# Rows of y in groups of four steps, and transposes with TensorE's transpose flag, in a state-space layer with a gated feed-forward

## The chip, the cores and the metric

The kernel runs on one core of a Trainium2 chip. The metric is the device time of one execution in microseconds (us). TensorE, VectorE, ScalarE and GpSimd each have their own instruction stream and meet by semaphores; in the profile they are PE (its weight loads PEld), DVE, ACT and POOL, and SP only issues transfers.

## The reference, cut to what matters

Two sequences of 1024 steps, width D = 512, state N = 128 per channel; the feed-forward has 2048 hidden units.

```
xn = rmsnorm(x) * norm_w;  xn = xn * sigmoid((xn @ select_w.T + b) * gate)
delta, B, C = split(xn @ x_proj_w.T);  delta = softplus(delta @ dt_w.T + dt_b)
for each step:  h = exp(delta * A) * h + (delta * xn) outer B;  y = h . C
x = layernorm(x + (y + x * D_param) @ out_w.T)
x = layernorm(x + (silu(x @ w_gate.T) * (x @ w_up.T)) @ w_down.T)
```

The scan over steps is the only sequential part: h of one step needs h of the step before.

## The kernel before, in words

All data are float32. The 128 partitions hold the state index N; the free axis holds the two sequences times 512 channels, so h of one step is 128 x 1024 in a ring of seven slots (`H_RING = 7`). The 1024 steps are cut into 8 chunks of 128 (`TB`), and into blocks of four steps (`BS = 4`).

- VectorE (line 693 on) runs the recurrence. Per step and sequence it multiplies `a` (the decay) by the h before into PSUM (`m_ps`, L708), and adds the input term into the next slot of h (L728 where the input term was scaled beforehand, L731 where this is part of the same instruction). Before it writes h of step t it waits at L713 for `s_y >= t - H_RING + 1`, that is for the row of y of step t-7, because that row reads the slot to be overwritten.
- TensorE gives the exponents: `exponents(q)` (L1214, matmuls at L1223) spreads delta times A for half a block into four PSUM banks, and ScalarE takes the exponential from there into `a` (L1004). Its places are in the table `P_AT`, one at every odd step. It needs ScalarE to have read the one before.
- TensorE gives the rows of y: `y_row(t)` (L1287) multiplies h of step t by a column of C placed so that the result falls into one row of `y_ps`; four column groups of the array are used, two by even and two by odd steps. It waits for h of its own step and adds one to `s_y`. A float32 matmul leaves two records, so two steps have eight records of L1299.
- Everything else is hung on the steps by `timetable`: for each half step a list of pieces of the chunk before (output projection, layer norm, gate and up products, down product) and of the chunk after (the projections that give delta, B, C). TensorE issues the pieces of a half step behind the exponents and the rows of y placed there, strictly in that order, so a wait in one holds up all that follows. Sixteen windows of 64 steps are projected and normalised; ScalarE copies `y_ps` at the second step behind each window, and the first row of the next window waits for that; windows of y (`yt`) and of the first norm's output (`vt`) are transposed by four matmuls against the identity (L1123 and L1163).
- Weights stream from HBM through `w_ring`, each load issued by ScalarE when TensorE has used up the slot; SP issues the broadcast of the input term of each step (`u_bc`).
- After the last step the second half of the last chunk is finished alone (the tail), in which VectorE does the norms and copies.

Of the kernel before, what the change touches and what calls it, by code (L numbers as in the profile page):

```python
# [5 lines left out]
BATCH, SEQ, D, N, R, HID = 2, 1024, 512, 128, 128, 2048  # L6
# [11 lines left out]
BS = 4  # L18
# [175 lines left out]
def build(nc, xT, x_rows, vecs, d_row, sel_wT, xproj_wT, dt_wT, out_wT, A_log, gu_w, down_w, out_rows):  # L194
# [5 lines left out]
    with ctx:  # L200
# [855 lines left out]
        def tensor(e):  # L1056
# [52 lines left out]
            def behind(x, stage, j):  # L1109
                cols = columns_of(x)  # L1110
                if stage == "yt":
# [6 lines left out]
                    for k in range(KB):  # L1118
                        if x > LAST and k % PAIR == 0:
                            e.wait_ge(s_y2, k // PAIR + 1)  # L1120
                        part = dst if x <= LAST else final_half(stage, x, j, k // PAIR)
                        at = k if x <= LAST else k % PAIR
                        last = e.matmul(part[:, at * P:(at + 1) * P], v(x, j)[:, k * P:(k + 1) * P], ident[:, :], start=True,  # L1123
                                        stop=True)
                        if x > LAST and k % PAIR:
                            last.then_inc(s_yt2, 1)
                    if x <= LAST:
# [24 lines left out]
                elif stage == "vt":  # L1152
# [3 lines left out]
                    for k in range(KB):  # L1156
                        if x > LAST and k == 0:
                            e.wait_ge(s_nm, 1)
                        elif x > LAST and k == PAIR:
                            e.wait_ge(s_work, emptied("outp", x, j))  # L1160
                        part = dst if x <= LAST else final_half(stage, x, j, k // PAIR)
                        at = k if x <= LAST else k % PAIR
                        last = e.matmul(part[:, at * P:(at + 1) * P], v(x, j)[:, k * P:(k + 1) * P], ident[:, :], start=True,  # L1163
                                        stop=True)
                        if x > LAST and k % PAIR:
                            last.then_inc(s_vt2, 1)
                    if x <= LAST:
# [13 lines left out]
                elif stage == "down":  # L1181
# [13 lines left out]
                    for i in range(HB // 4):  # L1195
                        hb = part * (HB // 2) + sub * (HB // 4) + i
                        if m == 0:
                            e.wait_ge(s_gated, HB // 2 * x + hb // 2 + 1)
                        last = e.matmul(dst, tile[:, sub * (HB // 4) + i, :], hidden(x, hb), start=hb == 0,  # L1199
                                        stop=hb == HB - 1)  # L1200
# [86 lines left out]
            def y_row(t):  # L1287
                blk, i = t // CS, t % WIN // 2
                if t == 0:
                    e.wait_ge(s_ucp, BATCH * FIRST_U)  # L1290
                elif t % WIN == 0:
                    e.wait_ge(s_ycp, t // WIN)
                e.wait_ge(s_cz, blk + 1)
                e.wait_ge(s_h, BATCH * (t + 1))
                for b in range(BATCH):
                    entry = (blk % CZ_RING * BATCH + b) * CS + t % CS
                    first = GP * entry + GP - 1 - i
                    group = 2 * (t % 2) + b
                    last = e.matmul(y_ps[group * GP:(group + 1) * GP, :], cz[:, first:first + GP],  # L1299
                                    h[:, t % H_RING, b * D:(b + 1) * D], start=i == 0, stop=i == GP - 1)  # L1300
                last.then_inc(s_y, 1)

            first_chunk()
            for t in range(SEQ):
                c = t // TB
                for i in range(SLOTS):
                    if SLOTS * t + i in P_AT:
                        exponents(P_AT[SLOTS * t + i], p_ps)
                    if i == 0 and t % 2 == 0 and t:
                        y_row(t - 2)  # L1310
                        y_row(t - 1)
                    for stage, x, j in plans[c].get(SLOTS * (t % TB) + i, ()):
                        behind(x, stage, j)
                        before(x, stage, j)
            y_row(SEQ - 2)
            y_row(SEQ - 1)
            e.wait_ge(s_exp, TILES_P)
            for slot in sorted(plans[CHUNKS]):
                for stage, x, j in plans[CHUNKS][slot]:
# [50 lines left out]
```

## Time and profile before

| | us |
|---|---|
| three timed runs | 2670.43, 2664.76, 2670.15 (median 2670.15) |
| span of the profiled execution, first to last instruction | 2662.4 |
| the profiled execution's time around its span | not given by the page; the runs lie 2.4 to 8.0 above the span |
| VectorE busy / TensorE busy / ScalarE busy / GpSimd busy | 2577.2 / 2323.3 / 1836.4 / 1030.8 |
| scan, first step to last step | 37.4 to 2599.4 |
| tail behind it | 63 |

Times are from the start of the span. Busy shares are averages over stages with different limits; a row of the timeline has its start, its duration, the engine, the line, what is written and read, the count of merged records, and in brackets the idle time of the engine before it with what ended it. The granted clock of TensorE has two levels, full (2.4 GHz) and half (1.2 GHz).

### The profile page before, as it was taken

To read this page: it belongs to the slowest core of one execution; us is meant where nothing else is said; L and a number is where in the kernel's file an instruction comes from. 1 tells how busy PE (TensorE), PEld (TensorE's weight loads), DVE (VectorE), ACT (ScalarE), POOL (GpSimd) and SP (SyncE) were. 2 spreads that over 40 slices of the span, in tenths; PEclk is the share of its full clock that TensorE was granted. 3 is DMA by queue.
4 is the path that set the end of the run, shared out by engine and by line. 5 is a ranking of instruction groups with operands and counts; after the bars stand their busy time and mean duration, and the time that the engine had idled before them with its cause. 6 is when DMAs were issued, how large, how long until landed. Compare 5 with 4: busy or idle time off the path is not lost.

```text
span 2662.4 us, 48762 instructions
## 1 busy us (share of the span) xinstructions
PE 2323.3 (87%) x17036; PEld 1281.6 (48%) x17036; DVE 2577.2 (97%) x4160; ACT 1836.4 (69%) x2432; POOL 1030.8 (39%) x1031
## 2 busy tenths in 40 slices
PE   7867678999789987899889998899978998998898
PEld 4322234545345544555445553454534554465557
DVE  6999999999999999999999999999999999999892
ACT  5778767678676776667766777767867678653743
POOL 2343333443344433444334433344334443343320
PEclk8999999999899998999999999999989999999999
DMA  5666666777667776777767787677766777787784
GB/s 189 216 215 223 225 237 238 276 257 275 239 243 272 269 270 228 252 268 276 264 231 264 258 287 246 233 278 257 271 245 231 272 265 268 264 289 281 246 323 156
DMA packets 192064, 672.20 MB, mean 252 GB/s; under 512 B 20944, under 2 KB 26064, under 8 KB 191824
## 3 DMA queue, kind: packets, MB, share of 16 engines
q1 hardware_dynamic: 152432, 544.02, 57.8%
q10 hardware_dynamic: 39392, 125.06, 13.8%
q8 instruction: 140, 2.29, 0.3%
q14 instruction: 100, 0.82, 0.1%
HBM read 660.61 MB, written 8.39 MB: 251 GB/s over the span
## 4 chain that ended last, share of the span: by engine, by line
PE 45%; DVE 25%; ACT 14%; issue 11%; DMA 4%; DVEq 0%; ACTq 0%; POOL 0%; POOLq 0%
PE banks L1059 14%; PE banks L1223 11%; DVE h L731 11%; PE banks L1299 9%; DVE banks L708 9%; PE banks L1199 8%; ACT a L1004 6%; DVE h L728 5%; DMA U<-in_xT 2%; ACT L742 1%; ACT u_bc L1023 1%; DMA u_bc<-u_scratch 1%; PE banks L1151 1%; PE banks L1147 1%; DMA w_ring<-in_down_w 1%
## 5 line engine op out<-in xcount | busy, mean ns | idle before, releaser
L708 DVE TENSOR_TENSOR banks<-a,h 128x512 f32<-128x512 f32 x2048 | 1331.5, 692 | 6.9 <-ACT a L1004 6.9
L1004 ACT ACTIVATE a<-banks 128x2048 f32<-128x2048 f32 x512 | 960.3, 1876 | 510.1 <-PE banks L1223 464.8
L731 DVE SCALAR_TENSOR_TENSOR h<-u_bc,BCt,banks 128x512 f32<-128x512 f32 x1285 | 899.0, 734 | 5.9 <-PE banks L1299 5.8
L603 POOL TENSOR_TENSOR dexp<-spread,dt 128x512 f32<-128x512 f32 x512 | 538.5, 1052 | 815.2 <-DVE banks L708 765.7
L1299 PE MATMUL banks<-h,cz 128*32 128x512 f32 x4096 | 696.7, 618 | 97.6 <-DVE h L728 50.0
L1223 PE MATMUL banks<-dexp,A 32*128 32x256 f32 x8192 | 612.1, 414 | 149.6 <-ACT a L1004 147.8
L1223 PEld LDWEIGHTS banks<-dexp,A 32*128 32x128 f32 x8192 | 383.9, 191 | 474.7 <-ACT a L1004 354.5
L728 DVE TENSOR_TENSOR h<-u_bc,banks 128x512 f32<-128x512 f32 x763 | 489.8, 674 | 3.3 <-POOL u_bc L615 3.3
L1059 PE MATMUL banks<-vT,w_ring 128*128 128x256 f32 x1792 | 453.2, 396 | 18.7 <-ACT up L971 17.6
L1059 PEld LDWEIGHTS banks<-vT,w_ring 128*128 128x128 f32 x1792 | 326.0, 192 | 187.7 <-issue 108.8
L1023 ACT ACTIVATE u_bc<-u_bc,BCt 128x512 f32<-128x512 f32 x497 | 333.2, 713 | 61.7 <-DMA u_bc<-u_scratch 60.9
L615 POOL TENSOR_SCALAR u_bc<-u_bc,BCt 128x512 f32<-128x512 f32 x266 | 184.0, 692 | 379.7 <-DVE banks L708 379.7
L1299 PEld LDWEIGHTS banks<-h,cz 128*32 128x32 f32 x4096 | 109.0, 109 | 382.5 <-issue 370.0
L1199 PE MATMUL banks<-gated,w_ring 128*128 128x256 f32 x896 | 225.1, 394 | 16.0 <-ACT vT L976 8.9
L1199 PEld LDWEIGHTS banks<-gated,w_ring 128*128 128x128 f32 x896 | 162.1, 191 | 100.1 <-issue 65.4
L969 ACT ACTIVATE sg<-banks 128x256 f32<-128x256 f32 (+1 forms) x144 | 51.8, 360 | 143.4 <-PE banks L1059 141.9
L543 POOL TENSOR_TENSOR gated<-gated,sg 128x512 f32<-128x512 f32 x56 | 75.0, 1340 | 96.1 <-DVE banks L708 75.5
L546 POOL TENSOR_TENSOR gated<-gated,up 128x512 f32<-128x512 f32 x56 | 72.5, 1294 | 78.3 <-DVE banks L708 78.3
L742 ACT ACT_TABLE_LOAD x55 | 70.6, 1283 | 14.5 <-issue 12.3
L1059 PE MATMUL banks<-U,w_sel 128*128 128x256 f32 x256 | 70.5, 425 | 8.3 <-ACT dt L770 7.1
L973 ACT ACTIVATE sg<-sg,half 128x256 f32<-128x256 f32 (+1 forms) x144 | 71.4, 496 | 0.0
L1059 PEld LDWEIGHTS banks<-U,w_sel 128*128 128x128 f32 x256 | 51.2, 210 | 34.6 <-issue 15.7
(179 smaller groups left out, 1276.1 us busy)
## 6 DMA issues: line engine op xcount, KB each, us to landing
u_bc<-u_scratch SPq DMA_DIRECT2D x1021, 512.0 KB, 4.6
w_ring<-in_gu_w ACTq DMA_DIRECT2D x112, 512.0 KB, 5.0
w_ring<-in_down_w ACTq DMA_DIRECT2D x56, 512.0 KB, 5.3
a<-in_gu_w ACTq DMA_DIRECT2D x16, 512.0 KB, 5.6
a<-in_down_w ACTq DMA_DIRECT2D x8, 512.0 KB, 4.6
x_tok<-in_x_rows SPq DMA_DIRECT2D x15, 256.0 KB, 4.8
out_rows<-v ACTq DMA_DIRECT2D x15, 256.0 KB, 4.2
U<-in_xT ACTq DMA_DIRECT2D x7, 512.0 KB, 7.0
```

The source lines that it names most:

```text
L603: e.tensor_tensor(dexp[:, q % E_RING, :, :, :], spread[:, :].unsqueeze(1).unsqueeze(1).to_broadcast(shape), by_step[:, :, first:first + BS ...
L615: e.tensor_scalar(part, part, BCt[c % 2][:, 0, tl:tl + 1], 1.0, ALU.mult, ALU.mult).then_inc(s_zp, 1)
L708: e.tensor_tensor(m_ps[:, b, :], a[:, blk % A_RING, b, s, :], h[:, (t - 1) % H_RING, b * D:(b + 1) * D], ALU.mult).then_inc(s_m, 1)
L728: e.tensor_tensor(h[:, t % H_RING, part], u_bc[:, t % U_RING, part], m_ps[:, b, :], ALU.add).then_inc(s_h, 1)
L731: e.scalar_tensor_tensor(h[:, t % H_RING, part], u_bc[:, t % U_RING, part], BCt[c % 2][:, 0, b * TB + tl:b * TB + tl + 1], m_ps[:, b, :], ...
L742: e.preload_act_table_set("natural_log_exp_and_others")
L1004: e.activation(dst.rearrange("p b t (x j) -> p x (b t) j", j=GP), src.rearrange("p g (i r j) -> p (g i) r j", i=PAIR, j=GP), ACT.Exp, scal ...
L1023: e.activation(part, part, ACT.Copy, scale=BCt[c % 2][:, 0, b * TB + tl:b * TB + tl + 1]).then_inc(s_za, 1)
L1059: last = e.matmul(dst, w, x, start=i == 0, stop=i == len(pairs) - 1)
L1199: last = e.matmul(dst, tile[:, sub * (HB // 4) + i, :], hidden(x, hb), start=hb == 0, stop=hb == HB - 1)
L1223: last = e.matmul(dst[:, g, i * COLS:(i + 1) * COLS], A[rows, q % 2 * PAIR + i, :], lays, start=True, stop=True)
L1299: last = e.matmul(y_ps[group * GP:(group + 1) * GP, :], cz[:, first:first + GP], h[:, t % H_RING, b * D:(b + 1) * D], start=i == 0, stop=i ...
```

## The change

Line 1309 issued the rows of steps t-2 and t-1 at each even step t. Now the rows of the last four steps (`BS = 4`) are issued at each step t that is a multiple of four, and the last four rows behind the loop. The matmuls that transpose a window of y (L1123) and of the first norm's output (L1163) get the flag `is_transpose=True`; other products with the identity stay as they are.

```diff
@@ the transposes of y, and in the same way those of the first norm's output
-                        last = e.matmul(part[:, at * P:(at + 1) * P], v(x, j)[:, k * P:(k + 1) * P], ident[:, :], start=True,
-                                        stop=True)
+                        last = e.matmul(part[:, at * P:(at + 1) * P], v(x, j)[:, k * P:(k + 1) * P], ident[:, :], start=True,
+                                        stop=True, is_transpose=True)
@@ the loop of TensorE over the steps
                     if SLOTS * t + i in P_AT:
                         exponents(P_AT[SLOTS * t + i], p_ps)
-                    if i == 0 and t % 2 == 0 and t:
-                        y_row(t - 2)
-                        y_row(t - 1)
+                    if i == 0 and t % BS == 0 and t:
+                        for gone in range(t - BS, t):
+                            y_row(gone)
                     for stage, x, j in plans[c].get(SLOTS * (t % TB) + i, ()):
                         behind(x, stage, j)
                         before(x, stage, j)
-            y_row(SEQ - 2)
-            y_row(SEQ - 1)
+            for gone in range(SEQ - BS, SEQ):
+                y_row(gone)
```

## Rows read from the trace of the kernel before

**Rows 1.** Page: the span, and busy time (share) and instructions of each engine.

```profile
span 2662.4 us, 48762 instructions
PE 2323.3 (87%) x17036; PEld 1281.6 (48%) x17036; DVE 2577.2 (97%) x4160; ACT 1836.4 (69%) x2432; POOL 1030.8 (39%) x1031
```

**Rows 2.** Page, costliest groups: busy, mean ns of one, idle before and releaser.

```profile
L1299 PE MATMUL banks<-h,cz 128*32 128x512 f32 x4096 | 696.7, 618 | 97.6 <-DVE h L728 50.0
```

**Rows 3.** Waits of VectorE, whole span: us in total, times, longest.

```profile
DVE moments L563 <- PE banks L1210: 14.9, 1, 14.9
DVE h L731 <- PE banks L1299: 5.8, 3, 4.8
```

**Rows 4.** Timeline of TensorE: chunk 7, then a place where rows stand together.

```profile
2307.62 1.07 PE L1299 MATMUL banks<-h,cz 128*32 128x512 f32 x8
2308.62 1.99 PE L1059 MATMUL banks<-vT,w_ring 128*128 128x256 f32 x8
...
2582.46 3.10 PE L1299 MATMUL banks<-h,cz 128*32 128x512 f32 x16
```

**Rows 5.** Timeline of VectorE and TensorE at the scan's start.

```profile
56.67 1.40 DVE L731 SCALAR_TENSOR_TENSOR h<-u_bc,BCt,banks 128x512 f32<-128x512 f32 x2
...
56.92 1.94 PE L1299 MATMUL banks<-h,cz 128*32 128x512 f32 x8
```

**Rows 6.** The same two engines at the start of chunk 2.

```profile
716.82 1.39 DVE L731 SCALAR_TENSOR_TENSOR h<-u_bc,BCt,banks 128x512 f32<-128x512 f32 x2
...
718.40 1.08 PE L1299 MATMUL banks<-h,cz 128*32 128x512 f32 x8
...
726.60 1.39 DVE L731 SCALAR_TENSOR_TENSOR h<-u_bc,BCt,banks 128x512 f32<-128x512 f32 x2
...
728.74 1.07 PE L1299 MATMUL banks<-h,cz 128*32 128x512 f32 x8
```

**Rows 7.** The same in chunk 3.

```profile
1045.55 1.40 DVE L731 SCALAR_TENSOR_TENSOR h<-u_bc,BCt,banks 128x512 f32<-128x512 f32 x2
...
1046.48 1.07 PE L1299 MATMUL banks<-h,cz 128*32 128x512 f32 x8
```

**Rows 8.** The same in chunk 6.

```profile
1999.40 1.40 DVE L731 SCALAR_TENSOR_TENSOR h<-u_bc,BCt,banks 128x512 f32<-128x512 f32 x2
...
2001.63 1.06 PE L1299 MATMUL banks<-h,cz 128*32 128x512 f32 x8
```

**Rows 9.** The same in chunk 4.

```profile
1361.51 1.06 PE L1299 MATMUL banks<-h,cz 128*32 128x512 f32 x8
...
1365.24 1.39 DVE L731 SCALAR_TENSOR_TENSOR h<-u_bc,BCt,banks 128x512 f32<-128x512 f32 x2
```

**Rows 10.** Busy time by stretch, two chunk starts; the granted clock is behind POOL's.

```profile
684.00:720.00 36.00, 28.66 (x181) 13.57 (x182) 36.00 (x59) 21.44 (x26) 13.81 (x15) 0.81 0.62 219
1320.00:1356.00 36.00, 29.34 (x210) 14.51 (x210) 36.00 (x59) 22.61 (x29) 13.69 (x15) 0.95 0.65 220
```

**Rows 11.** Timeline of VectorE and TensorE in the second half of chunk 7.

```profile
2455.60 1.41 DVE L731 SCALAR_TENSOR_TENSOR h<-u_bc,BCt,banks 128x512 f32<-128x512 f32 x2 [4.79 <-PE banks L1299]
...
2460.37 1.06 PE L1299 MATMUL banks<-h,cz 128*32 128x512 f32 x8
...
2501.08 1.39 DVE L731 SCALAR_TENSOR_TENSOR h<-u_bc,BCt,banks 128x512 f32<-128x512 f32 x2
...
2505.23 1.07 PE L1299 MATMUL banks<-h,cz 128*32 128x512 f32 x8
...
2506.95 0.69 DVE L728 TENSOR_TENSOR h<-u_bc,banks 128x512 f32<-128x512 f32 x1 [3.26 <-POOL u_bc L615]
```

**Rows 12.** Groups of TensorE in the tail, 2599 to 2612: the two transposes.

```profile
L1163 PE MATMUL banks<-ident,v 128*128 128x128 f32 x8 | 1.2, 288 | 2.1 <-DVE v L568 2.1
L1123 PE MATMUL banks<-ident,v 128*128 128x128 f32 x8 | 1.1, 275 | 0.0
```

More of the change, by code:

```diff
@@ L1163, in behind @@
                         last = e.matmul(part[:, at * P:(at + 1) * P], v(x, j)[:, k * P:(k + 1) * P], ident[:, :], start=True,
-                                        stop=True)
+                                        stop=True, is_transpose=True)
                         if x > LAST and k % PAIR:
```

## The prediction

> **What bounds the kernel now.** The page comes first: VectorE is busy for 2577.2 us of a span of 2662.4, TensorE for 2323.3 [rows 1]. The scan is a recurrence: each of the 1024 steps is two products and two additions on VectorE, which follow each other without a gap. Its waits come next. In the whole span VectorE loses 5.8 us to TensorE's rows of y, in three places, and the largest single wait, 14.9 us, is for the last product behind the scan [rows 3]. So the scan is bound by VectorE, and TensorE matters in three ways only: where its lag behind the scan grows so large that VectorE has to wait, in chunk 7 (steps 896 to 1023), where it is packed solid, and in the tail of 63 us after the last step.
>
> What a reader must count is the lag that VectorE tolerates. The ring of h has seven slots, so the write of step t needs the row of y of step t-7. I number the steps by counting VectorE's pairs of writes, and the rows of y by counting eight matmul records for two steps (a float32 matmul leaves two records).
>
> **The change part by part.**
>
> *Rows in fours.* Nothing is added or removed: still 1024 rows, 4096 records [rows 2]. What moves is the place of rows 4k and 4k+1 in TensorE's order: from the head of step 4k+2 to the head of step 4k+4. Rows 4k+2 and 4k+3 stay at step 4k+4, behind the other two.
>
> (a) TensorE's own time. Two steps' rows cost 1.00 us where they stand alone between other work (2307.62 to 2308.62 [rows 4]). The only place where four steps' rows stand together mixes them with waits and shows 3.10 us for 16 records [rows 4], so it gives no cheaper price than twice 1.07. I bound the saving by nothing and by 0.2 us for four steps, and take 0.12, since a lone group ends in a drain that a following one can cover. Over 256 groups that is 31 us of TensorE time, but it is off the path except in bursts, where two to twelve groups count: 0.3 us each, 1.5 us in chunk 7.
>
> (b) The new tightest wait. Row 4k is needed by the write of step 4k+7. It used to be issued at the head of step 4k+2, five steps ahead, and is now issued at the head of 4k+4, three steps ahead. Where TensorE keeps up that is harmless: three steps are about 7.5 us and the row takes 1. Where TensorE lags, VectorE will stop. The test for each k: the time at which the old trace shows the rows of 4k+2 starting (the place to which row 4k moves) plus 1.0 us, against the start of the write of step 4k+7. If the first is later, VectorE waits for the difference.
>
> - Start of the scan: rows 2 and 3 start at 56.92 and take 1.94 us, since the clock is at half there; the write of step 7 starts at 56.67 [rows 5]. Wait 56.92+1.94-56.67 = 2.2 us.
> - Chunk 2, first: 718.40+1.0 against the write of step 275 at 716.82: 2.6 us. Second: 728.74+1.0 against 726.60: 3.1 us [rows 6]. Waits in one burst are not added, since VectorE's delay of the first is slack for the second; the largest counts.
> - Chunk 3: 1046.48+1.0 against 1045.55: 1.9 us [rows 7].
> - Chunk 6: 2001.63+1.0 against 1999.40: 3.2 us [rows 8].
> - Chunk 4: 1361.51+1.0 against 1365.24: 2.7 us to spare [rows 9]; chunks 1 and 5 look the same. The chunks differ in the granted clock around the start of their first products: 0.81 from 684 to 720 in chunk 2, 0.95 from 1320 to 1356 in chunk 4 [rows 10].
>
> (c) The push. Four rows now stand ahead of the other work of step 4k+4, which is 0.88 us later (one more pair), and that of 4k+2 is 1.0 us earlier. At the chunk starts the piece behind 4k+4 feeds a chain over ScalarE (product, tanh, next product) to the next late row, so in chunks 2, 3 and 6 the wait may grow by 0.9 us, to 4.0, 2.8 and 4.1. On the other side, row pair 4k, taken away at 4k+2, may pull the late row forward by up to 1.0 us: 2.1, 0.9 and 2.2, and 1.1 at the start. Queued behind the wait on VectorE is the whole recurrence, so each such us is one of the span. With the push, start and chunks 2, 3 and 6 sum to 2.2+4.0+2.8+4.1 = 13.1; without it and with the pull, to 1.1+2.1+0.9+2.2 = 6.3.
>
> (d) Chunk 7. VectorE waits 4.79 us for a row at 2455.60 because TensorE lost time to a weight load, and later at 2506.95 for GpSimd, which is late by the same lag [rows 11]. By the test, row 964 would come at 2460.37+1.0 in place of 2455.60, 5.8 us later, and row 980 at 2505.23+1.0 against a write at 2501.08, 5.2 us. But the stop at 2506.95 is set by TensorE's lag and not by VectorE, so it swallows nearly all of this: a write that starts at 2506.2 lets the next step's begin at 2506.2+2.5 = 2508.7, against 2506.95, which is 1.8 us. From this goes the 1.5 us that TensorE has saved by then. I take +0.5, with -1.5 and +4 as ends, since the load and ScalarE's turns are reordered with it.
>
> (e) What gets earlier for TensorE. It stops for h at every fourth step only, so the work of steps 4k+2 and 4k+3 no longer stands behind a wait. VectorE isn't helped by that: it waits for nothing from that work outside chunk 7.
>
> *The transpose flag.* Fourteen of the fifteen windows' transposes lie beside the scan and save TensorE time off the path. In the tail both transposes stand on the path: 1.1 and 1.2 us for 8 records each [rows 12]. The second half of each overlaps nothing, the first is partly covered by VectorE's copies. No transpose with the flag is in this trace: the bounds are -1.6 us (both nearly free on the path) and +1 us (if it is slower than a plain one); I take -0.7, nearer to the middle of the gain.
>
> The trace shows a plain float32 transpose at 288 ns a record [rows 12]. The Trainium skill, page "TensorE: Matmul & The Clock Gate", table "Terms", says that the transpose mode makes float32 four times as fast; by that the tail would save some 1.6 us in place of 0.7. No row here shows it.
>
> **Sum.** With the push: 13.1+0.5-0.7-0.9 (grouping saved in three bursts) = 12.0. With the pull: 6.3+0.5-0.7-0.9 = 5.2. Nothing in the rows decides between the two for all chunks, since in chunk 2 the first late row follows a stop for ScalarE (pull void) and in the others the work is denser; I take the middle, +8.6. The profiled execution has a span of 2662.4; the page gives no time around it, and the three timed runs lie 2.4 to 8.0 above it. 2662.4+8.6 = 2671.0 of span, and on the median of 2670.15 the forecast is 2678.8 us.
>
> **The rivals.**
>
> *Every chunk start gets cold (slower, more).* TensorE now has its rows in a lump and up to 4 us of lighter load after it, so the granted clock may be at half at the starts of chunks 1, 4 and 5 too [rows 10]. Each would then lose what chunks 2, 3 and 6 lose, about 3: 8.6+9 = +18, 2688 us. For it: the clock falls at each chunk start already, only for different lengths. Against: the load there is set by ScalarE's pace more than by the rows.
>
> *The lag disappears (no change).* If the freed waits and the cheaper groups let TensorE enter the bursts ahead, the late rows come up to 2.5 us earlier. Then the waits of chunks 2, 3 and 6 fall to 1 or less and only the start costs 1 to 2: +1 to +3, 2672 us. For it: TensorE stops for h before the bursts at present. Against: the late rows stand behind chains over ScalarE, not behind TensorE's own work.
>
> *Chunk 7 heals (faster).* In chunk 7 VectorE loses some 15 us in stops, all born of TensorE's lag when the weight load is issued. If TensorE comes to that load 2 us or more ahead, and its transfer doesn't collide with those behind it, the stops shrink by 8 to 12 us, which is more than the waits at the chunk starts: about -5, 2665 us. It decides from 7 us saved in chunk 7 on. Against: from 2307 on TensorE saves only 0.12 us a group.
>
> *The transposes cool the clock.* Work at half clock takes about twice as long (two steps' rows 1.94 us against 1.07 [rows 4, 5]). The tail's products behind the second transpose run at the full clock now; I allow 4 us for a stretch of them at half: +12 in all. The Trainium skill, page "TensorE: Matmul & The Clock Gate", section "Part 4: PE-mode transpose", says that transposes in this mode do not count as activity for the clock; no row here shows it, and it is one reason for this rival.
>
> **How the numbers follow.** Forecast (+5 to +12) 0.42; every start cold 0.15; lag disappears 0.22; chunk 7 heals 0.15; transposes cool 0.06. About 0.2% of the time, 5.3 us, is what a measurement of this kernel can tell from no change. Of the forecast's 0.42 a fifth lies under +5.3, with the rival "lag disappears": same 0.31. Faster 0.14, slower 0.55. The range goes from 2664 (chunk 7 healed in part) to 2691 (starts cold).
>
> **What would show it.** In the profile of the changed kernel VectorE's wait for the rows of y should rise from 5.8 us [rows 3] to some 12 to 25, in few long waits within 60 us of the starts of chunks 2, 3 and 6 and near the scan's start, all at steps 4k+7. The step (a) is wrong if eight more records cost 1.0 us; (c) if the waits are above 4.1 or under 2; (d) if the stop near 2507 is gone. The forecast is wrong if TensorE's rows never come later than the write they free, or if the waits also appear in chunks 1, 4 and 5.

## The result, and the profile after

The changed kernel takes 2682.62 us in the median of 20 runs (2665.25 to 2691.58), the kernel before 2668.81 in the median of its 20 (2658.23 to 2673.85). The ratio is 1.0043 with a 95% interval of 1.0028 to 1.0058, so +11.5 us (7.5 to 15.5). The profiled execution took 2682.14 us at a span of 2680.3, that is 1.8 us around the span. Its span is 17.9 us above that of [rows 1]. That is more than the medians differ, because the profile before is of one of the shorter executions of its kernel: with 1.8 us around it the span of 2662.4 makes 2664.2 us, 4.6 under the median of 2668.81, while the profile after lies at its median. Three executions (one of the kernel before at 3235 us and two of e12 below at 5307 and 7555) belong to a slower state and are in no ratio, which leaves e12 four.

The page of the kernel after, first the span with the busy times, then two groups (busy, mean ns of one, idle before and its releaser):

```profile
span 2680.3 us, 48506 instructions
PE 2274.6 (85%) x16908; PEld 1305.5 (49%) x16908; DVE 2571.7 (96%) x4160; ACT 1835.1 (68%) x2432; POOL 1027.7 (38%) x1031
...
L731 DVE SCALAR_TENSOR_TENSOR h<-u_bc,BCt,banks 128x512 f32<-128x512 f32 x1285 | 901.4, 737 | 30.1 <-PE banks L1299 29.9
...
L1299 PE MATMUL banks<-h,cz 128*32 128x512 f32 x4096 | 617.6, 646 | 38.8 <-DVE h L731 24.0
```

TensorE has 128 records fewer (each of the 128 transposes, two sets of sixteen windows of four, now leaves one in place of two), is busy for 48.7 us less than in [rows 1], and the same 4096 records of rows of y take 79 us less than in [rows 2]. VectorE does the same work and is busy for 5.5 us less. It is longer only by what it waits for. Its waits, in us in total, times, longest:

```profile
DVE h L731 <- PE banks L1299: 29.9, 9, 9.2
DVE gated L543 <- ACT sg L973: 26.1, 8, 7.3
DVE moments L563 <- PE banks L1210: 14.9, 1, 14.9
...
DVE banks L708 <- ACT a L1004: 4.1, 2, 3.2
```

The wait for rows of y has gone from 5.8 us in three places to 29.9 in nine; the wait behind the scan for the last product is still 14.9, as in [rows 3]. The span divides into three parts: the start up to the first step 40.6 us (37.4 before), the scan 2574.3 (2562.0), the tail 65.4 (63.0). The change does not touch the start, and across the kernels below it lies anywhere from 37.4 to 41.2 in one execution, so its 3.2 us are scatter. What is to be explained is the 12.3 us of the scan and the 2.4 of the tail.

The timeline of the kernel after, TensorE's rows of y and the write of VectorE that they release, at the start, in chunk 4, in chunk 6 and twice in chunk 7 (start, duration, and in brackets idle time before and what ended it):

```profile
61.90 3.64 PE L1299 MATMUL banks<-h,cz 128*32 128x512 f32 x16
63.92 1.40 DVE L731 SCALAR_TENSOR_TENSOR h<-u_bc,BCt,banks 128x512 f32<-128x512 f32 x2 [3.37 <-PE banks L1299]
...
1360.01 1.93 PE L1299 MATMUL banks<-h,cz 128*32 128x512 f32 x16
1361.17 1.41 DVE L731 SCALAR_TENSOR_TENSOR h<-u_bc,BCt,banks 128x512 f32<-128x512 f32 x2 [2.03 <-PE banks L1299]
...
1366.93 1.15 PE L1223 MATMUL banks<-dexp,A 32*128 32x256 f32 x16 [2.00 <-ACT a L1004]
...
1372.85 1.92 PE L1299 MATMUL banks<-h,cz 128*32 128x512 f32 x16
...
2002.70 1.41 DVE L731 SCALAR_TENSOR_TENSOR h<-u_bc,BCt,banks 128x512 f32<-128x512 f32 x2 [2.99 <-PE banks L1299]
...
2015.51 1.41 DVE L731 SCALAR_TENSOR_TENSOR h<-u_bc,BCt,banks 128x512 f32<-128x512 f32 x2 [2.94 <-PE banks L1299]
...
2473.60 1.41 DVE L731 SCALAR_TENSOR_TENSOR h<-u_bc,BCt,banks 128x512 f32<-128x512 f32 x2 [9.24 <-PE banks L1299]
...
2509.84 1.41 DVE L731 SCALAR_TENSOR_TENSOR h<-u_bc,BCt,banks 128x512 f32<-128x512 f32 x2 [5.59 <-PE banks L1299]
```

The reader is to see the pattern: sixteen records (four steps' rows) begin late, and 1.2 us after their start (2.0 us at the half clock of the start), when the first of the four rows is done, VectorE writes. By the count of VectorE's writes these are steps 7, 531, 535, 787, 791, 971 and 983, all of the form 4k+3, that is the 4k+7 of the forecast. Two more, at steps 407 in chunk 3 and 979, are of 0.4 us. Before, such stops were at 971 (4.8 us) and hardly elsewhere.

Where TensorE's clock stands, in windows of the two kernels (length, busy time and count of PE, PEld, DVE, ACT, POOL, then granted clock, DMA share, GB/s); the first three rows are of the kernel after, and the fence behind them has the first stretch of the kernel before:

```profile
100.00:340.00 240.00, 164.96 (x1246) 67.30 (x1246) 240.00 (x395) 184.47 (x215) 91.54 (x97) 0.84 0.65 220
684.00:720.00 36.00, 28.62 (x210) 13.80 (x202) 36.00 (x59) 26.19 (x33) 14.42 (x15) 0.87 0.71 251
1320.00:1356.00 36.00, 26.01 (x182) 11.97 (x182) 36.00 (x58) 24.36 (x30) 13.85 (x15) 0.78 0.73 252
```

```profile
100.00:340.00 240.00, 170.64 (x1262) 63.88 (x1262) 240.00 (x396) 186.75 (x218) 93.19 (x99) 0.97 0.63 221
```

In the light stretch from 100 to 340 TensorE is busy for 5.7 us less although many of its instructions run slower, and the granted clock falls from 0.97 to 0.84. At the start of chunk 4 it goes from 0.95 [rows 10] to 0.78, at that of chunk 2 from 0.81 to 0.87. Over the span the mean granted clock is 0.936 in place of 0.968; counted as time at 1.2 GHz, (1-clock) x 2 x span, that is 343 us in place of 170.

### The profile page after: what moved, and what is told of

Same layout as the page of the kernel before. It is cut to its first block, busy times and chain, and to the rows that moved or that the text cites. A ratio compares the mean times of both kernels' runs of the same rounds, so it can differ in the third digit from the quotient of the medians.

```text
span 2680.3 us, 48506 instructions
## 1 busy us (share of the span) xinstructions
PE 2274.6 (85%) x16908; PEld 1305.5 (49%) x16908; DVE 2571.7 (96%) x4160; ACT 1835.1 (68%) x2432; POOL 1027.7 (38%) x1031
## 3 DMA queue, kind: packets, MB, share of 16 engines
q10 hardware_dynamic: 39392, 125.06, 13.7%
## 4 chain that ended last, share of the span: by engine, by line
DVE 41%; PE 27%; issue 14%; ACT 12%; DMA 5%; DVEq 1%; ACTq 0%; POOL 0%; POOLq 0%
DVE h L731 17%; DVE banks L708 15%; PE banks L1059 9%; DVE h L728 9%; PE banks L1223 7%; PE banks L1299 6%; ACT a L1004 5%; PE banks L1199 3%; DMA u_bc<-u_scratch 3%; ACT u_bc L1023 1%; ACT L742 1%; DMA U<-in_xT 1%; DMA w_ring<-in_down_w 1%; DVEq L727 0%; ACT v L884 0%
## 5 line engine op out<-in xcount | busy, mean ns | idle before, releaser
L731 DVE SCALAR_TENSOR_TENSOR h<-u_bc,BCt,banks 128x512 f32<-128x512 f32 x1285 | 901.4, 737 | 30.1 <-PE banks L1299 29.9
L1223 PE MATMUL banks<-dexp,A 32*128 32x256 f32 x8192 | 634.5, 427 | 265.9 <-ACT a L1004 259.3
L1223 PEld LDWEIGHTS banks<-dexp,A 32*128 32x128 f32 x8192 | 394.1, 196 | 538.6 <-ACT a L1004 412.0
L1299 PE MATMUL banks<-h,cz 128*32 128x512 f32 x4096 | 617.6, 646 | 38.8 <-DVE h L731 24.0
L1059 PE MATMUL banks<-vT,w_ring 128*128 128x256 f32 x1792 | 436.0, 390 | 15.6 <-ACT up L971 15.6
L1299 PEld LDWEIGHTS banks<-h,cz 128*32 128x32 f32 x4096 | 127.1, 115 | 380.9 <-issue 376.1
L543 POOL TENSOR_TENSOR gated<-gated,sg 128x512 f32<-128x512 f32 x56 | 71.6, 1279 | 82.7 <-DVE banks L708 76.6
L1059 PE MATMUL banks<-U,w_sel 128*128 128x256 f32 x256 | 80.8, 473 | 7.3 <-ACT dt L770 6.3
L742 ACT ACT_TABLE_LOAD x55 | 70.6, 1283 | 14.5 <-issue 12.3
L1059 PEld LDWEIGHTS banks<-U,w_sel 128*128 128x128 f32 x256 | 57.9, 236 | 35.5 <-issue 15.3
```

Of the source, the lines that this page charges most:

```text
L731: e.scalar_tensor_tensor(h[:, t % H_RING, part], u_bc[:, t % U_RING, part], BCt[c % 2][:, 0, b * TB + tl:b * TB + tl + 1], m_ps[:, b, :], ...
L742: e.preload_act_table_set("natural_log_exp_and_others")
L1059: last = e.matmul(dst, w, x, start=i == 0, stop=i == len(pairs) - 1)
L1223: last = e.matmul(dst[:, g, i * COLS:(i + 1) * COLS], A[rows, q % 2 * PAIR + i, :], lays, start=True, stop=True)
```

## The experiments

Twelve kernels ran, with 4 to 12 executions each that count. Ratios are against the kernel before, with 95% intervals; clock, waits, stops and tails are from one profiled execution of each. The diffs are cut to the lines that matter. "Stops" and "slower instructions" are my count from VectorE's instructions in the scan of the profiled execution: whatever the distance between two starts has above the normal 0.60 us (0.60 or 0.66 for the two forms of the write); it is a stop where the instruction before had ended, and otherwise the instruction itself ran longer.

| kernel | ratio (interval) | clock | wait for rows, us | stops / slower instructions, us |
|---|---|---|---|---|
| before | 1 | 0.968 | 5.8 | 13.7 / 12.5 |
| after | 1.0043 (1.0028 to 1.0058) | 0.936 | 29.9 | 32.2 / 6.4 |
| e1 fours only | 1.0043 (1.0030 to 1.0056) | 0.936 | 28.1 | 29.9 / 7.2 |
| e2 flag only | 1.0005 (0.9995 to 1.0016) | 0.959 | 3.6 | 11.0 / 18.3 |
| e4 pairs, two steps later | 1.0062 (1.0046 to 1.0078) | 0.925 | 37.1 | 41.2 / 9.7 |
| e7 one row each step | 1.0381 (1.0359 to 1.0403) | 0.971 | 9.0 | 45.9 / 95.3 |
| e8 fours, TensorE filled up | 1.0209 (1.0193 to 1.0224) | 0.953 | 52.3 | 55.6 / 29.3 |
| e11 pairs, 7 slots, lean | 1.0021 (1.0001 to 1.0040) | 0.961 | 2.0 | 9.7 / 20.3 |
| e6 fours, 7 slots, lean | 1.0042 (1.0026 to 1.0057) | 0.938 | 17.7 | 22.1 / 13.3 |
| e5 pairs, 8 slots, lean | 1.0030 (1.0019 to 1.0041) | 0.966 | 2.0 | 14.7 / 18.2 |
| e3 fours, 8 slots, lean | 1.0024 (1.0010 to 1.0037) | 0.938 | 3.8 | 16.6 / 13.5 |
| e10 pairs, 8 slots | 0.9999 (0.9985 to 1.0012) | 0.959 | 0 | 8.0 / 18.3 |
| e9 fours, 8 slots | 1.0050 (1.0033 to 1.0066) | 0.930 | 13.6 | 21.3 / 13.2 |
| e12 pairs at the chunk starts, fours elsewhere | 1.0067 (1.0046 to 1.0087) | 0.938 | 8.5 | 17.5 / 25.5 |

In this count the kernel after loses 24.1 us more to rows of y than the kernel before, 5.6 less in other stops and 6.1 less in slower instructions: together the 12.3 us of the scan. Slower instructions are 12.5 to 20.3 us in the kernels with pairs at their old places, and stops 8.0 to 14.7, so a difference of a few us between two single profiles says nothing.

**The two parts alone.** e1 has the new loop with plain transposes:

```diff
-                    if i == 0 and t % 2 == 0 and t:
-                        y_row(t - 2)
-                        y_row(t - 1)
+                    if i == 0 and t % BS == 0 and t:
+                        for gone in range(t - BS, t):
+                            y_row(gone)
```

> Rows of y in fours, plain transposes. Theory A (the late rows): the write of step 4k+7 waits for row 4k wherever TensorE lags, so this alone gives nearly the whole loss: ratio 1.004 (about 2680 us), VectorE's wait for the rows of y 20 to 30 us as in the changed kernel (29.9). Rival B (the transpose flag makes the loss, through the clock): ratio 1.000 to 1.001, wait under 10 us. Granted clock: if the lumps of rows cool TensorE, the mean stays near 0.936; if the flag does it, it returns to 0.968.

Measured: 1.0043, as the whole change, with the same clock and the same waits. e2 has the old loop with the flag:

```diff
-                                        stop=True)
+                                        stop=True, is_transpose=True)
```

> Rows of y in pairs as before, transposes with the flag. Theory A: no change in the scan, VectorE's wait for the rows 5 to 8 us; the transposes have half the records and save under 1 us in the tail: ratio 0.999 to 1.001. Rival B: ratio 1.003 or more, granted clock under 0.95. A third reading (the flag costs only in the tail, where the products behind the second transpose then run at half clock, 6.9 us in place of 4.5 for 38 records): ratio 1.001, tail 2 us longer.

Measured: 1.0005, an interval that holds 1, and a clock of 0.959 as other kernels with pairs have it (e10 0.959, e11 0.961). So the fours make the whole loss, and the flag moves nothing that can be measured. Tail of e1 and of e2: 64.0 us each, between before's 63.0 and after's 65.4.

**Late, but not in lumps.** e4 keeps pairs and issues each two steps later, so that row 4k comes at the same step as in the fours, and row 4k+2 later than there:

```diff
-                    if i == 0 and t % 2 == 0 and t:
-                        y_row(t - 2)
-                        y_row(t - 1)
+                    if i == 0 and t % 2 == 0 and t > 2:
+                        y_row(t - 4)
+                        y_row(t - 3)
```

> Rows still in pairs at every even step, but two steps later than before (rows t-4 and t-3 at step t), so that each pair's first row has the same three steps to its deadline as row 4k in fours, with no lumps and no lighter stretches between. Theory A, lateness alone: VectorE waits as much as in the fours, 15 to 30 us, ratio 1.003 to 1.006. Rival C (lateness hurts only together with the half clock that the lumps bring): granted clock back to 0.96 to 0.97, wait 8 to 15 us (the stops of chunks 2, 3 and 6 that the old trace predicts, without the ones in further chunks), ratio 1.000 to 1.003.

Measured: 1.0062, more than the fours. The expected return of the clock to 0.96 or more did not come. No row stands in a lump, yet VectorE waits for rows in 18 places. The waits and one window of e4:

```profile
DVE h L731 <- PE banks L1299: 37.1, 18, 8.3
...
100.00:340.00 240.00, 154.26 (x1242) 65.09 (x1238) 240.00 (x396) 184.91 (x214) 91.75 (x97) 0.80 0.63 220
```

The lump is not what costs. What e4 and the fours share is the later place, and with it, which I had not reckoned with, a less busy TensorE and a lower clock: 154.3 us busy in the light stretch, at 0.80.

**Early singles.** e7 issues each row one step behind its h:

```diff
-                    if i == 0 and t % 2 == 0 and t:
-                        y_row(t - 2)
-                        y_row(t - 1)
+                    if i == 0 and t:
+                        y_row(t - 1)
```

> One row of y per step, at every step, plain transposes. Each row stands alone, so the two column groups of the other step's row lie idle and the TensorE time of the rows rises (theory: about 0.9 us a row in place of 0.5, some 400 us more in all), while lateness is the least possible. Theory A: deadlines alone would give a ratio of 0.998 to 1.000, but the dearer rows make TensorE lag in chunk 7 and at the chunk starts: ratio 1.01 to 1.05. If the clock is what matters, the mean granted clock rises above 0.97.

Measured: 1.0381, with the highest clock of all, 0.971. A row alone occupies two of the four column groups and costs TensorE as much as two rows do (rows below, step (e)); here every row goes alone, in the bursts and in chunk 7 too. Its waits for rows are small (9.0 us), and the loss is paid elsewhere: 92 of GpSimd's products take over 1.45 us (11 before), and VectorE's own instructions are longer by 95 us, nearly all of it beside such products; it also stops 24 us for input terms that GpSimd and ScalarE have not yet scaled. So a high clock alone makes nothing fast.

**Is it the deadline?** If the late row alone were the cause, an eighth slot for h, which moves the deadline one step (2.5 us) back, should take most of the loss. The memory is full, so something has to go. In e3, e5, e6 and e11 ("lean") the ring of the products that GpSimd makes ahead has three places in place of four, and the tile of `D_param` is left out and a row of `w_out` read in its place, so the output is not the reference's. e6 and e11 are the controls with seven slots.

```diff
-H_RING = 7
+H_RING = 8
-E_RING = 4
+E_RING = 3
-        d_skip = sb("d_skip", [P, D])
-                e.tensor_tensor(v(x, j), x_tok(x, j), d_skip[:, :], ALU.mult).then_inc(s_xd, 1)
+                e.tensor_tensor(v(x, j), x_tok(x, j), w_out[:, 0, :], ALU.mult).then_inc(s_xd, 1)
```

> The same (the product with D_param replaced, too) with eight slots of h: row 4k is needed by the write of step 4k+8, one step (2.5 us) later, while the lumps and the half clock stay. Theory A (the deadline makes the stops): the stops at chunk starts, 2 to 4 us each, shrink to 0 to 1.5, chunk 7's by some 3, so VectorE's wait falls from about 28 to 8 to 15 us and the ratio to 1.000 to 1.002, at a granted clock still near 0.936. Rival C (the half clock costs by other ways, such as ScalarE's and GpSimd's lag): ratio stays at 1.003 or above, with other waits of VectorE in its place.

> Control for the next two kernels. Rows in fours, plain transposes, seven slots of h, and on-chip memory freed for an eighth: the ring of delta's spread is three slots deep in place of four, and D_param has no tile of its own, so the product with D_param is made with a row of the output projection's weights (that part of the computation is thereby replaced). All theories: as the fours with nothing freed, ratio 1.003 to 1.006, VectorE's wait for the rows of y 20 to 30 us. If the shallower ring matters, it shows here as waits of VectorE for the decay a.

> Rows in pairs as before, eight slots of h, memory freed in the same way (the product with D_param replaced). Theory A: in pairs only chunk 7's stop of 4.8 us and smaller ones go, and chunk 7's later stops for a and for GpSimd set the end as before, so 0 to 3 us faster: ratio 0.999 to 1.000. If lateness in chunk 7 were all, ratio 0.997 and under.

> Control for the eight-slot pairs: rows in pairs, seven slots, delta's spread in a ring of three, the product with D_param replaced by one with a row of the output projection's weights. If the shallower ring is what made the eight-slot pairs 0.3% slower than the kernel before, this is at ratio 1.002 to 1.004 too, with VectorE waiting for GpSimd for some 10 us; if the eighth slot itself did it, 1.000.

Measured: fours 1.0042 with seven slots and 1.0024 with eight; pairs 1.0021 and 1.0030. With seven slots the intervals of the two overlap; with eight the fours lose nothing against the pairs. Taken alone this would say that the eighth slot heals the fours, and VectorE's wait for rows has indeed gone to 3.8 us. But the lean ring costs the pairs 0.2 to 0.3% by itself (e5 had been expected at 0.999 to 1.000) and brings a wait of its own, for GpSimd (fours with eight slots; 3.3 in the kernel before):

```profile
DVE h L726 <- POOL u_bc L613: 9.3, 7, 5.5
```

So the pair was made again without the lean ring. e10 (pairs) and e9 (fours) have eight slots and four places; `D_param` and the weights of the projection to delta are taken from rows of `w_out`, so their output is not the reference's, and a buffer of the last chunk is moved.

```diff
-H_RING = 7
+H_RING = 8
-        w_dt = sb("w_dt", [P, D])
+        w_dt = w_out[:, 1, :]
-            return w_dt[:, :] if x == LAST else ymod[:, :]
+            return ymod[:, :]
```

> The same with rows in fours and plain transposes. Theory A (the whole loss is the deadline of row 4k): with a step more to it the fours are as fast as the pairs with eight slots, within 0.1%, though the granted clock stays near 0.936; VectorE's wait for the rows falls from 28 us to under 8. Rival C (lower clock and lag cost in other ways): 0.2% or more slower than the eight-slot pairs, with waits for GpSimd or for a in place of those for the rows.

> Rows in pairs, eight slots of h, delta's spread in its ring of four as before; the room comes from D_param's tile and from the weights of the delta projection (both products are made with rows of the output projection's weights, so these two parts are replaced), and the window's transpose of y in chunk 7 uses the common buffer. Theory A: no row is late, chunk 7's stop of 4.8 us is partly paid elsewhere: ratio 0.998 to 1.000.

Measured: pairs 0.9999, so the slot and the memory for it cost nothing; fours 1.0050. The wait for rows is down to 10.9 + 2.7 = 13.6 us, less than half of after's 29.9, and the loss is still there in full. The waits of e9, for rows in the first and the last line:

```profile
DVE h L725 <- PE banks L1294: 10.9, 5, 4.5
DVE banks L705 <- ACT a L999: 7.8, 4, 2.9
...
DVE h L728 <- PE banks L1294: 2.7, 4, 0.8
```

This does not acquit the late row. In e10 VectorE waits for no row at all, so against its control e9 still loses 13.6 us to rows, now to row 4k for the write of step 4k+8, and that is as much as its stops have grown (21.3 against 8.0). The expectation that one slot more would bring the wait under 8 us was wrong; that the loss would then take another form is not shown by this pair. Where the wait did go, in e3, the fours cost nothing against their control. Why the lean fours with eight slots do better than e9 (1.0024 against 1.0050) I can't say.

**Filling TensorE up again.** To raise the clock of the fours without moving a row, e8 adds at steps 4k+2 of chunks 0 to 6 four products with zero weights, which go into the open sum of `y_ps` and change nothing there:

```diff
+                    if i == 0 and t % BS == 2 and t % WIN > 2 and c < LAST:
+                        for g in range(G):
+                            e.matmul(y_ps[g * GP:(g + 1) * GP, :], nought[:, :], w_out[:, g, :], start=False, stop=False)
```

> Rows in fours, plain transposes, and at the steps 4k+2, where the pairs were issued before, four matmuls of weights zero added to the rows' bank (they add zeros; chunk 7 has none, nor the second step of a window). TensorE is as busy again as with pairs. Theory A: the granted clock goes back to 0.96 or more, but row 4k is as late as in fours, so the stops at the starts of chunks 2 to 6 stay for the chunks where the clock is low at the start, and some added work in the bursts makes them larger: ratio 1.003 to 1.007. Rival C (the clock is what makes the loss): ratio 1.000 to 1.002 and VectorE's wait under 18 us.

Measured: 1.0209, outside what either reading expected. (The first such step of each window of 64 has no filling.) The clock rises to 0.953 and not to the pairs' 0.96, and VectorE waits 52.3 us for rows: it seems that the added work delays TensorE in the bursts by more than the clock gives back. The filling is too dear to isolate the clock, and the run decides nothing on it.

**Rows at their old places where the bursts are.** e12 has pairs in the first 40 steps of each chunk and in chunk 7, where all stops of [rows 6 to 9] and of chunk 7 lie, and fours in between:

```diff
-                    if i == 0 and t % 2 == 0 and t:
-                        y_row(t - 2)
-                        y_row(t - 1)
+                    if i == 0 and t and (t % BS == 0 or t % 2 == 0 and (c == LAST or t % TB < 40)):
+                        for gone in range(t - 2 if paired or t % BS == 2 else t - BS, t):
+                            y_row(gone)
+                        paired = t % BS == 2
```

> Rows in pairs, at their old places, in the first 40 steps of each chunk and in all of chunk 7; in fours everywhere else; plain transposes, seven slots. The light stretches, in which most of the half clock of the changed kernel lies, stay as in the fours; the bursts, where TensorE lags, are as before. Theory A (the loss is made where a late row meets a lagging TensorE): VectorE's wait for the rows is back to 5 to 10 us and the ratio to 0.999 to 1.001, though the granted clock stays at 0.94 to 0.95. Rival C (the half clock of the light stretches is what costs, by putting TensorE behind when a burst begins): ratio 1.002 or more, with stops at the starts of chunks.

Measured: 1.0067. The wait for rows is nearly back at its old size:

```profile
DVE h L731 <- PE banks L1299: 8.5, 5, 3.2
```

and the kernel is slower than with fours throughout. With hardly a row late, what is left of the change is the fours in the light stretches: there the clock is 0.88 from 100 to 340 in place of before's 0.97, and TensorE enters the bursts behind. By the start of a block's last rows against their h, its largest lag near the starts of chunks 1 to 6 is 6.3, 13.2, 12.5, 12.5, 12.8 and 14.9 us. Pairs have 5.1, 11.0, 10.6, 5.1, 5.2 and 11.1 in the kernel before, and 6.3, 10.1, 12.4, 10.6, 11.7 and 11.1 in e2, so from chunk 2 on e12 is above both, by much or by little. The lag now reaches VectorE by another way. At step 27 of each of the chunks 2 to 6 GpSimd's product at L496 waits for TensorE's exponents and then runs beside VectorE's products of step 28. Chunk 4 of e12, then the same place in the kernel before:

```profile
1381.52 1.84 POOL L496 TENSOR_TENSOR U<-U,dt 128x512 f32<-128x512 f32 x1 [2.37 <-PE banks L1223]
1381.54 2.38 DVE L708 TENSOR_TENSOR banks<-a,h 128x512 f32<-128x512 f32 x2
```

```profile
1375.37 1.27 POOL L496 TENSOR_TENSOR U<-U,dt 128x512 f32<-128x512 f32 x1 [1.41 <-DVE banks L708]
1376.52 1.29 DVE L708 TENSOR_TENSOR banks<-a,h 128x512 f32<-128x512 f32 x2
```

VectorE's pair takes 2.38 us in place of 1.29. This costs e12 1.1 us in each of five chunks, the kernel before nothing, and e2 1.1 us once. A dearer meeting, of a pair with two of GpSimd's products in turn at step 36, is not e12's own: it stands there in four chunks (2, 3, 4, 6), in e2 in three and in the kernel before in two (3 and 6). Chunk 3 of e12, then of the kernel before:

```profile
1079.14 1.29 DVE L708 TENSOR_TENSOR banks<-a,h 128x512 f32<-128x512 f32 x2
1079.37 2.18 POOL L543 TENSOR_TENSOR gated<-gated,sg 128x512 f32<-128x512 f32 x1 [5.32 <-ACT sg L973]
1081.66 3.13 DVE L708 TENSOR_TENSOR banks<-a,h 128x512 f32<-128x512 f32 x2
1082.52 1.71 POOL L546 TENSOR_TENSOR gated<-gated,up 128x512 f32<-128x512 f32 x1
```

```profile
1076.70 3.14 DVE L708 TENSOR_TENSOR banks<-a,h 128x512 f32<-128x512 f32 x2
1077.58 1.71 POOL L546 TENSOR_TENSOR gated<-gated,up 128x512 f32<-128x512 f32 x1
```

All such slower instructions cost e12 25.5 us, the kernel before 12.5 and e2 18.3; the rest of e12's loss is in stops (17.5 us against 13.7 and 11.0). So both of the readings on record missed a part: the ratio is that of rival C, but the stops at the chunk starts that it named are few. And since e12 loses more than the fours throughout, it shows a second way for a loss and not how much of the first kernel's loss took it. In the kernel after slower instructions cost 6.4 us, less than in any kernel with pairs.

## Why the forecast came out as it did

The forecast was 2678.8, +8.6 us, with 2664 to 2691. Measured are 2682.62, +13.8 by the medians and +11.5 by the ratio. The sign, the range and the place (VectorE waiting for rows of y) hold; the size was some 3 to 5 us short, and one step is missing from the working. That the sum came so near is in part luck: the waits for rows grew by 24.1 us, to 29.9 where 12 to 25 had been named, and 11.7 us came back, 5.6 in other stops, of which (d) has only the one near 2507, and 6.1 in slower instructions, of which the forecast has nothing. One of its own signs of being wrong has also come: waits in chunk 4. Step by step:

- **(a) The price of a group.** Where TensorE is packed solid the kernel after shows

```profile
2324.48 1.92 PE L1299 MATMUL banks<-h,cz 128*32 128x512 f32 x16
2326.33 1.99 PE L1059 MATMUL banks<-vT,w_ring 128*128 128x256 f32 x8
```

  so four steps' rows cost 1.85 us from start to start against 2 x 1.00 [rows 4]: 0.15 saved, taken 0.12. The term holds there. But the total, "31 us over 256 groups", is far off: the busy time of the rows fell by 79 us, against a clock that was lower.

- **(b) The late row.** The form holds: each stop is for a group of sixteen records at a step 4k+7, its size about 3 us (2.0, 3.0, 3.0, 2.9, and 3.4 at the start, foreseen 1.9 to 3.2). The places don't: chunk 4 has two stops and was foreseen to have 2.7 us to spare, chunks 2 and 3 have none above 0.4 and were foreseen to have 1.9 to 3.1. The test took TensorE's order of one execution as fixed. Its lag at a chunk start differs from one execution to the next, as the granted clock there does: chunk 4 fell from 0.95 to 0.78, chunk 2 rose from 0.81 to 0.87. Even the same loop puts the stops elsewhere: e1 has 0.86 from 1320 to 1356, where after has 0.78, and stops also in chunks 2 and 5. And it is not the fours alone that moved it: e2, with pairs, has 0.85 in that window and a largest lag of 10.6 us near the start of chunk 4, where the kernel before has 0.95 and 5.1. The 2.7 us to spare were those of one execution. From one trace the test gives the size of a stop and how many starts are near it, not which ones.

- **(c) Push or pull.** No stop at a chunk start is above 4.1, and none under 2 but the one of 0.4 in chunk 3. The sum over the starts is 3.4 + 2.0 + 3.0 + 3.0 + 2.9 = 14.3, nearer to the sum with the push (13.1) than to the middle that I took (9.7). Against that stands a gain that I had not looked for: VectorE's slower instructions beside GpSimd fell from 12.5 to 6.4 us (12.5 to 20.3 in the kernels with pairs). By steps of the scan it comes to +12.3, where the forecast had 9.7 + 0.5 - 0.9 = 9.3. That the waits of one burst don't add up was wrong here: in chunks 4 and 6 both stops of a burst stand in full. In chunk 4 the exponents between the two stand behind ScalarE (the row at 1366.93 above, idle for 2.00 us), so the second group came late again whatever VectorE had lost.

- **(d) Chunk 7.** Its excess over the normal pace goes from 17.1 to 19.2 us, +2.1 where I took +0.5 with ends -1.5 and +4. The stop at step 971 grew from 4.8 to 9.2 us and the one near 2507 remains, now for a row of y (5.6 us) and not for GpSimd; the stops for ScalarE (3.6 us) and for GpSimd (3.3) that followed in the kernel before are gone. So most of the rows' delay was swallowed, as (d) has it, and the sum is within the ends; the stop at 971 grew by 4.4 us where the test gave 5.8.

- **(e) What gets earlier.** This step fell short, by omission. I wrote that the removed waits for h don't help VectorE, and asked nothing more of them. Under pairs TensorE stops for h at every even step of a light stretch and leaves its rows one by one. The timeline of the kernel before, and then of the kernel after, in the same stretch:

```profile
262.83 1.05 PE L1299 MATMUL banks<-h,cz 128*32 128x512 f32 x4 [0.27 <-DVE h L728]
265.23 1.05 PE L1299 MATMUL banks<-h,cz 128*32 128x512 f32 x4 [1.35 <-DVE h L728]
```

```profile
269.19 2.46 PE L1299 MATMUL banks<-h,cz 128*32 128x512 f32 x12
271.96 1.05 PE L1299 MATMUL banks<-h,cz 128*32 128x512 f32 x4 [0.31 <-DVE h L728]
```

  One step's four records cost 1.05 us, as much as two steps' eight records (1.07, [rows 4]). Packed, as in the kernel after, rows seldom stand alone. The pairs keep TensorE busy by work done badly, and at 2.4 GHz; the fours make it less busy, and the granted clock falls to 0.84 there. What the light stretch hands to the burst is then a lower clock, and in e12 also a larger lag. In the kernel after the lag itself is not shown to be larger: its largest near the starts of chunks 1 to 6 is 7.3, 7.7, 9.0, 11.6, 8.0 and 11.8 us, above the kernel before in four of six but no higher on the whole than e2. This is in part the rival "every chunk start gets cold": right in that the clock falls more often, wrong in the size (+18, 2688) and in that all starts would be alike. How much of the missing 3 to 5 us is this step's can't be separated from (c).

- **The transposes.** With the flag a group of four transposes leaves four records. The tail of e2 (first two lines), then that of the kernel after:

```profile
2607.24 0.60 PE L1123 MATMUL banks<-ident,v 128*128 128x128 f32 x4
2614.12 0.92 PE L1163 MATMUL banks<-ident,v 128*128 128x128 f32 x4 [2.15 <-DVE v L568]
```

```profile
2618.64 0.64 PE L1123 MATMUL banks<-ident,v 128*128 128x128 f32 x4
2625.57 1.14 PE L1163 MATMUL banks<-ident,v 128*128 128x128 f32 x4 [2.15 <-DVE v L568]
2627.27 6.91 PE L1059 MATMUL banks<-vT,a 128*128 128x128 f32 x38 [0.56 <-DVE vT L573]
```

  Against 1.1 and 1.2 us [rows 12] that is about -0.5 and -0.3 in e2, at the taken -0.7. In after the second one runs at half clock and saves next to nothing, and the products behind it take 6.91 us for 38 records (4.48 before): here the tail lost the 2.4 us by which it is longer. The rival "transposes cool the clock" named this very place. Does the flag do it? Not by itself: the same 38 records take 6.11 us in e1, e4 and e9 and 5.95 in e12, all without the flag, at a mean clock of 0.79 over the 8 us from the start of the second transposes, where the kernel before and e10 have 1.00 and 4.48 us. With the flag they take 6.91 (after) and 7.37 (e2), and without it up to 6.59 (e5), so the half clock there needs no flag, and the flag's share, if it has one, is about 1 us. Over the scan the rival is out: e2's clock and time are those of pairs. The forecast counted fifteen windows; there are sixteen, fifteen of them beside the scan, which changes no term. The Trainium skill, page "TensorE: Matmul & The Clock Gate", table "Terms", has float32 four times as fast in transpose mode; the rows here show 0.60 us in place of 1.1, less than a factor of two.

- **The other rivals.** "The lag disappears" is out: the waits that it would have shortened grew. "Chunk 7 heals" is out: 17.1 to 19.2 us.

**What is shown, and what is only supported.** Shown: the fours make the loss and the flag doesn't (e1, e2). The lumps are not needed for it (e4). In the kernel after VectorE's whole excess stands in its waits for rows of y, at steps 4k+7 as foreseen; an eighth slot (e9) halves them and does not end them. Bringing the rows back to their old places in the bursts (e12) takes the wait for rows away and leaves a loss, so the late row is not the only way: TensorE's lag then reaches VectorE by collisions with GpSimd. Supported, not shown: that the lower clock adds to the lag. For it: the clock falls in the light stretch, where VectorE has no stop in either kernel, so there the stops did not bring it down; every variant that packs or delays rows without adding work has a clock of 0.925 to 0.938 and is slower than its control, clear of noise except in the lean pairs (overlapping intervals with seven slots, no loss with eight); over after's 20 runs the time falls with the mean granted clock (correlation -0.88; 2665 to 2671 us at 0.939 to 0.944 in four, 2683 to 2692 at 0.927 to 0.931 in eight), with code and order the same. Against it as the whole story: the fours reached 2665 us at a clock of 0.940, under the pairs' median of 2669 at a mean of 0.962, and a correlation doesn't tell what drives what. Open: no run raised the clock of the fours without adding work for TensorE, so clock and order stay mixed, and e3 against e9 is unexplained. No version beat both kernels; e10 equals the one before.

## What to carry to other kernels

When one engine sets the time, the order of work on an engine that feeds it is worth only what it does where that engine lags: test each moved piece against its deadline in the stretches where the feeder lags, and do not expect that one more buffer ends the loss, or that it ends when the pieces are back in place in the bursts alone (e9, e12). Before calling a row of one profile the cause, look for the same row in the kernel without the loss. Waits that are removed from TensorE, and work that is packed more densely, are not free gains: look at the granted clock in the light stretches ahead of each burst. Where the clock differs from one burst to the next, forecast how many stops of what size there will be, not in which burst.

## What the runs showed of the hardware

- One step's rows of y (four records on two column groups) cost TensorE 1.05 us, two steps' (eight records on four) 1.07, four steps' 1.92 (1.85 from start to start). Half-filled groups are paid in full, and e7, with every row alone, lost 3.8%.
- TensorE was granted less time at 2.4 GHz after its work became cheaper: 0.97 to 0.84 from 100 to 340 with 170.6 and 165.0 us busy, and 0.80 at 154.3 (e4). That is time saved on the engine's own work and a lower clock ahead of the bursts, in one move.
- A pair of VectorE's products with two inputs in on-chip memory takes 1.29 us alone and 2.38 beside one product of GpSimd with two inputs (1.84 us in place of 1.27), a price of 1.1 us on one meeting; with two of GpSimd's products in turn the pair takes 3.13, 1.8 us more. Either engine can pay: at 1079.14 in e12 the pair, which began first, takes its normal 1.29 and GpSimd's product 2.18, where the mean in the kernel after is 1.28 (71.6 us for 56). The Trainium skill, page "GPSIMD Engine Reference", section "8. Key points", names contention between the two for VectorE instructions with two such inputs; the rows agree.
